# Attention scores from 64 stacked rows per head instead of 128 with zeros, and the mask of the second tile added by VectorE

## What is computed

```
x = x + moe0(pool(x))          # layer 0: masked softmax pooling, 32 experts, 4 a token, and a shared one
y = x @ W[cat] + b[cat]        # layer 1: a matrix per item
q, k, v = split(layernorm(y) @ Wqkv);  q, k = rope(q), rope(k)          # 16 heads of 16
p = softmax(where(k_pos <= q_pos, q @ k.T / 4, -1e9))                   # 256 x 256 per head
y = y + (p @ v) @ Wproj
x = x + y + moe1(layernorm(y)) # 8 experts, 2 a token
```

## Time and profile before

| | us |
|---|---|
| median of 3 runs | 1647.37 (1645.69 to 1647.99) |
| the profiled execution, its own time | 1637.57 |
| its span in the profile | 1635.7 |

### The profile page before, as it was taken

How to read it: one execution, slowest core, us unless ns; L and a number is a source line. 1 busy time by engine, 2 the same in 40 slices (tenths; PEclk the granted TensorE clock), 3 DMA queues, 4 the chain that set the end, 5 groups by cost and what they waited for, 6 DMA issues and landing times.

```text
span 1635.7 us, 27557 instructions
## 1 busy us (share of the span) xinstructions
PE 1437.9 (88%) x9777; PEld 1248.5 (76%) x9777; DVE 1033.1 (63%) x2453; ACT 912.9 (56%) x2160; POOL 717.7 (44%) x712
## 2 busy tenths in 40 slices
PE   7988699999999997589869898889865999999996
PEld 5767599999999986466747666667654999999996
DVE  2998367766776757466756776768554555655552
ACT  5876255555555532267756676758744545554552
POOL 0787443344334114433453545644334444544443
PEclk9998799999999998799988998989876999999998
DMA  5410356555655531676575675676533223433312
GB/s 179 136 56 31 84 164 182 154 163 174 180 155 163 147 112 43 111 125 123 115 131 110 112 136 101 114 126 110 94 129 100 73 55 90 97 90 88 52 22 26
DMA packets 139448, 182.00 MB, mean 111 GB/s; under 512 B 22485, under 2 KB 107296, under 8 KB 139312
## 3 DMA queue, kind: packets, MB, share of 16 engines
q1 hardware_dynamic: 110512, 127.23, 31.3%
q0 software_dynamic: 28160, 51.96, 16.0%
q10 hardware_dynamic: 640, 1.05, 0.4%
HBM read 107.28 MB, written 42.08 MB: 91 GB/s over the span
## 4 chain that ended last, share of the span: by engine, by line
PE 67%; DVE 13%; issue 7%; another core or an unknown queue 7%; ACT 3%; POOL 2%; DMA 1%; SPq 1%; ACTq 0%; DVEq 0%; POOLq 0%
PE banks L942 41%; PE banks L1473 4%; PE banks L1430 4%; PE banks L451 3%; PE banks L1526 2%; PE banks L1004 2%; DVE hidden L977 2%; PE banks L1486 2%; PE banks L1447 1%; DVE lo_w L911 1%; DVE rm L1727 1%; DVE X L1695 1%; PE banks L1540 1%; DVE smax L1685 1%
## 5 line engine op out<-in xcount | busy, mean ns | idle before, releaser
L942 PE MATMUL banks<-hi_x,hi_w 128*128 128x320 f32 (+1 forms) x832 | 293.6, 353 | 35.0 <-DVE hidden L977 24.8
L942 PE MATMUL banks<-lo_x,hi_w 128*128 128x320 f32 (+1 forms) x832 | 288.5, 347 | 0.0
L942 PE MATMUL banks<-hi_x,lo_w 128*128 128x320 f32 (+1 forms) x832 | 288.2, 346 | 0.0
L942 PE MATMUL banks<-hi_w,hi_h 128*128 128x256 f32 x896 | 261.4, 292 | 5.9 <-issue 3.5
L884 POOL DMA_INDIRECT xe<-pooled,idx x160 | 155.5, 972 | 228.3 <-PE banks L1004 183.3
L942 PE MATMUL banks<-lo_w,hi_h 128*128 128x256 f32 x896 | 254.1, 284 | 0.0
L942 PE MATMUL banks<-hi_w,lo_h 128*128 128x256 f32 x896 | 254.0, 284 | 0.0
L942 PEld LDWEIGHTS banks<-hi_x,hi_w 128*128 128x128 f32 x832 | 160.2, 192 | 57.8 <-DVE hidden L977 29.7
L1878 POOL DMA_INDIRECT out<-X,tab x64 | 106.7, 1667 | 200.5 <-DVE X L1978 185.9
L1579 ACT ACTIVATE PN<-banks,smax 128x256 f32<-128x256 f32 (+1 forms) x512 | 180.2, 442 | 14.8 <-DVE smax L1685 13.8
L942 PEld LDWEIGHTS banks<-hi_w,hi_h 128*128 128x128 f32 x896 | 171.9, 192 | 7.6 <-issue 5.1
(11 more groups left out here) (186 smaller groups left out, 3101.0 us busy)
## 6 DMA issues: line engine op xcount, KB each, us to landing
w<-in_L_ffn_w SPq DMA_DIRECT2D x96, 256.0 KB, 5.6
done<-res SPq DMA_DIRECT2D x32, 640.0 KB
QS<-parts_qk SPq DMA_DIRECT2D x128, 128.0 KB
BIG<-in_L_ffn_W SPq DMA_DIRECT2D x16, 1024.0 KB
KS<-parts_qk SPq DMA_DIRECT2D x120, 128.0 KB
mask<-in_c_masks SPq DMA_DIRECT2D x16, 257.0 KB, 2.8
pooled<-XF SPq DMA_DIRECT2D x16, 256.0 KB, 3.3
WS<-in_L_cond_W SPq DMA_DIRECT2D x16, 256.0 KB
```

Source lines behind the costliest of these rows:

```text
L942: last = e.matmul(o, a[i], b[j], start=start and k == 0, stop=stop and k == 2, skip_group_check=True)
```

## The change

`KS` loses its second half and its zeros: head s has its 64 rows of `QS` and the same 64 rows of `KS`, and a score matmul works on these 64 rows alone (`half`). The two clearings by GpSimd and their semaphore go; the stacking of k waits in their place for the earlier users of that memory.

The parts are cut anew. Call 0 of a group now issues all scores of the second query tile, four matmuls of 256 columns, for the two heads of a pair alternately in the lower and upper rows, into banks 0 and 1; bank s holds the heads of half s. It has no mask matmul. Calls 1 and 2 each make half s of part 2: a mask matmul of 256 columns and two score matmuls of 128 columns. The head order of the values step follows.

For banks 0 and 1 VectorE adds a mask tile (`masks`, zeros for the first 128 keys and the triangle for the others), writes the negated sum to `PN` and takes its minimum, in one operation for each head. ScalarE's exponentials for these parts read and write `PN`, with scale -1. Call 0 waits for VectorE's four operations on the group before, not for ScalarE. In `PE_ROUND` three steps change places. The eight table entries of a routing group are issued four in each of two items.

```diff
     def stack(e, b, x):
-        if b < 2 and x == 1:
-            e.wait_ge(s_blocks, b + 1)
+        if b == 0 and x == 1:
+            e.wait_ge(s_xe_turned, 3 * E0)
+            for q in range(2):
+                e.wait_ge(s_res_out[q], 16 * (E0 // 2))
+        if b == 1:
             e.wait_ge(s_x_lo, x_count(NPT - 1, 1))
...
-                dst = KS[b % 2][rows_, s, :, :] if x else QS[b % 2][rows_, :, :]
+                dst = (KS if x else QS)[b % 2][rows_, :, :]
     def pe_scores(e, G, part):
-        if G >= 1:
-            e.wait_ge(s_pn, exp_count(G - 1, part))
-        if part < 2:
-            pair = 2 * g + part
-            e.matmul(PS[:, part, :]...[:, :, 1, :], ident_b[:, :], wide(causal[:, :], 1, [P, HQ, P]), start=True, ...)
-            last = e.matmul(PS[:, part, :], QS[b % 2][:, pair, P:T], KS[b % 2][:, :, pair, :], ...)
+        half = lambda t, s: t[b % 2][s * P // HQ:(s + 1) * P // HQ]
+        if part == 0:
+            if G >= 1:
+                e.wait_ge(s_smax, 5 * (G - 1) + 4)
+            for x in range(2):
+                for s in range(HQ):
+                    last = e.matmul(PS[:, s, x * T:(x + 1) * T], half(QS, s)[:, 2 * g + x, P:T], half(KS, s)[:, 2 * g + x, :], ...)
+                    if x == 1:
+                        last.then_inc(s_s[s], 1)
         else:
-            e.matmul(PS[:, 2, :]..., ident_b[:, :], wide(causal[:, :], 1, [P, HG, P]), start=True, ...)
+            s = part - 1
+            if s == 1:
+                e.wait_ge(s_s[2], 2 * G + 1)
+            elif G >= 1:
+                e.wait_ge(s_pn, exp_count(G - 1, 2))
+            e.matmul(PS[:, 2, s * T:(s + 1) * T]..., ident_b[:, :], wide(causal[:, :], 1, [P, 2, P]), start=True, ...)
             for x in range(2):
-                last = e.matmul(PS[:, 2, x * T:(x + 1) * T], QS[b % 2][:, pair, 0:P], KS[b % 2][:, :, pair, 0:P], ...)
+                last = e.matmul(PS[:, 2, (2 * s + x) * P:(2 * s + x + 1) * P], half(QS, s)[:, 2 * g + x, 0:P],
+                                half(KS, s)[:, 2 * g + x, 0:P], ...)
     act_attn, step exp
+                    if part < 2:
+                        e.wait_ge(s_smax, 5 * G + col + x + 1)
+                        e.activation(s, s, ACT.Exp, bias=smax[:, slot, col + x:col + x + 1], scale=-1.0).then_inc(s_pn, 1)
     dve_attn, step row_max
-                    e.wait_ge(s_pn, 8 * (G - NPN + 1))
+                    e.wait_ge(s_pt_ps, 3 * (G - NPN + 1))
+                if part < 2:
+                    for x in range(2):
+                        cols, col = slice(x * T, (x + 1) * T), 2 * part + x
+                        e.tensor_tensor_reduce(PN[:, slot, part, cols], PS[:, part, cols], masks[:, :], -1.0, 3.0e38,
+                                               ALU.add, ALU.min, smax[:, slot, col:col + 1]).then_inc(s_smax, 1)
     PE_ROUND: the order of the steps that move, before and after
-        ("scores", -1, 3, 0), ("turn_p", -1, 2, 2), ("scores", -1, 3, 1), ("values", -1, 1), ("norm_turn", 1),
-        ("turn_p", -1, 2, 0), ("turn_p", -1, 2, 1), ("gate_turn", -2),
+        ("scores", -1, 3, 0), ("turn_p", -1, 2, 2), ("values", -1, 1), ("norm_turn", 1),
+        ("turn_p", -1, 2, 0), ("turn_p", -1, 2, 1), ("scores", -1, 3, 1), ("gate_turn", -2),
-        ("scores", 0, 2, 1), ("matrix", 2),
+        ("matrix", 2), ("scores", 0, 2, 1),
     POOL_FIRST
-        (0, "blocks", 0), ... (0, "blocks", 1)
     pool_attn, step entry
-                for i in range(2 * d[0], 2 * d[0] + 2):     # two scatters a step, in the item where a group ends
+                g, i = entry_at(b, d[0])                    # one scatter a step, in that item and in the next
```

More of the change, by code:

```diff
@@ L126, in _build @@
     QS1 = sb("QS1", [P, NPAIR, T], F32R, place)
-    KS1 = sb("KS1", [P, HQ, NPAIR, T], F32R, place)
+    KS1 = sb("KS1", [P, NPAIR, T], F32R, place)
     place.close()
@@ L1223, in _build @@
     POOL_LAST = (
-        ("base", 14), ("entry", 14, 0), ("entry", 14, 1), ("entry", 14, 2), ("entry", 14, 3), ("norm", 15, 1),
-        ("base", 15), ("entry", 15, 0), ("entry", 15, 1), ("entry", 16, 0), ("entry", 16, 1))
+        *(("entry", 13, i) for i in range(TB * K1)), ("base", 14), *(("entry", 14, i) for i in range(R * K1)), ("norm", 15, 1), ("base", 15),
+        *(("entry", 15, i) for i in range(TB * K1)), *(("entry", 16, i) for i in range(TB * K1)))
     SP_LAST = (
@@ L1279, in group_ended, with entry_at @@
         return group_begun(b - 1) if b > 0 else None
+    def entry_at(b, i):
+        if group_ended(b) is not None:
+            return group_ended(b), i
+        return (group_ended(b - 1), TB * K1 + i) if group_ended(b - 1) is not None else None
     LBANK = 6
@@ L1326, in sp_attn @@
         wait_routed(e)
-        for dst, src in ((causal_f[:, :], io["c_causal"]),
+        for dst, src in ((masks[:, :], io["c_causal"]),
                          (wqkv[:, :, :], io["L1_ffn_WqkvT"].rearrange("(c p) f -> p c f", p=P)),
@@ L1390, in pool_attn @@
         for step, b, d in rounds(POOL_FIRST, POOL_ROUND, POOL_LAST):
[L1391 to L1395, removed]
+            if step == "got":
                 t, k = d
@@ L1413, in pool_attn @@
                                 ALU.add).then_inc(s_base, 1)
-            elif step == "entry" and group_ended(b) is not None:
-                g = group_ended(b)
-                t0 = r1.tiles(g)[0]
+            elif step == "entry" and entry_at(b, d[0]):
+                g, i = entry_at(b, d[0])
+                tt, k = r1.tiles(g)[0] + i // K1, i % K1
                 if d[0] == 0:
@@ L1440, in pe_scores @@
                 e.wait_ge(s_stack[x], N_STACK * (b + 1))
-        if G >= 1:
-            e.wait_ge(s_pn, exp_count(G - 1, part))
-        if part < 2:
-            pair = 2 * g + part
[L1445 to L1448, removed]
-        else:
-            e.matmul(PS[:, 2, :].rearrange("p (h k) -> p h k", h=HG), ident_b[:, :], wide(causal[:, :], 1, [P, HG, P]),
-                     start=True, stop=False, skip_group_check=True)
+        half = lambda t, s: t[b % 2][s * P // HQ:(s + 1) * P // HQ]
[4 more added lines that the diff above has]
+                for s in range(HQ):
+                    last = e.matmul(PS[:, s, x * T:(x + 1) * T], half(QS, s)[:, 2 * g + x, P:T], half(KS, s)[:, 2 * g + x, :],
+                                    start=True, stop=True, skip_group_check=True)
+                    if x == 1:
+                        last.then_inc(s_s[s], 1)
+        else:
+            s = part - 1
[3 more added lines that the diff above has]
+                e.wait_ge(s_pn, exp_count(G - 1, 2))
+            e.matmul(PS[:, 2, s * T:(s + 1) * T].rearrange("p (h k) -> p h k", h=2), ident_b[:, :],
+                     wide(causal[:, :], 1, [P, 2, P]), start=True, stop=False, skip_group_check=True)
             for x in range(2):
[L1453 to L1456, removed]
+                last = e.matmul(PS[:, 2, (2 * s + x) * P:(2 * s + x + 1) * P], half(QS, s)[:, 2 * g + x, 0:P],
+                                half(KS, s)[:, 2 * g + x, 0:P], start=False, stop=True, skip_group_check=True)
+            last.then_inc(s_s[2], 1)
     def pe_turn_p(e, G, part):
```

69 lines of the change are left out of this document (32 added, 37 removed).

## The result

The changed kernel took 1695.8 us (median of 4, 1692.5 to 1700.1) beside 1646.5 us for the kernel before in the same session: ratio 1.0305, 95% interval 1.0274 to 1.0336. It is slower by 49 us, twice the 24.5 us of the forecast and inside its range; the rival "all calls are paid" had 1689.

What follows compares the result with a forecast made beforehand. TensorE was taken to bound about half of each attention item. Paid work of 1.35 us plus VectorE's 0.18 made 1.53 us an item, 24.5 us over 16; added to 1647.37 that gave 1672 us, 8-in-10 range 1640 to 1703.

Steps and rivals of the forecast that it cites:

- all calls are paid: Rival: no score call's added TensorE work hides in idle time; 41 us slower, 1689 us; chance 0.10.
- New work on TensorE: Score calls in attention: a group costs 1.735 us against 1.13, so +0.60 us a group.
- A way in and out: TensorE going to 64-row matmuls and back at each score call: 0.325 us lost, ends 0.30 and 0.35.
- Pairs run at once: Call 0: matmuls on upper and lower rows overlap, streaming 0.22 us instead of 0.43.
- the rival without pairs: Rival: call 0's matmuls run one after the other, 0.43 us; +7 us, 1679 us; chance 0.14.
- the 0.27 of a recorded length: Alternative drain price for each of 24 added shape changes on TensorE: 0.27 us, 6.5 us an item.
- Which of it is paid: TensorE's added work: 1.35 us an item paid, 1.05 hidden in VectorE's stretch and the standstill.
- the granted clock: TensorE's clock in attention: a mean of 0.92 was read in the first window; no term priced a change.
- the whole forecast of 1.53: Added time an item in attention: 1.35 us of TensorE plus 0.18 of VectorE, 24.5 us over 16 items.
- VectorE and ScalarE: Attention row maxima and exponentials: VectorE's combined operations add 0.18 us an item on the chain, ScalarE nothing.
- The moved steps save none: TensorE's new round: 32 shape changes an item against 8, and moving steps avoids none of the added ones.
- GpSimd and the transfers: Removed key-tile clearings and moved table entries: worth nothing; without cover 7 us and some 5 us.

Runs made afterwards that it cites:

- the two balances: Profiles of the changed kernel against the kernel before, compared over fifteen items in two sessions: 1695.8 beside 1646.5 us, and 1697.8 beside 1649.3 us.
- the pair without a lower clock: Two variants of the changed kernel: every score matmul on 128 rows, 1508.6 us, and 64-row matmuls with TensorE's round from the kernel before, 1578.1 us.
- the extra one: The changed kernel with a small full-array matmul of 32 columns between the two pairs of call 0: 1559.4 us, ratio 1.0377 to the kernel before.
- all rows: The changed kernel with every score matmul on 128 rows, two heads' scores added up: 1509.2 us, ratio 1.0046 to the kernel before; run again, 1508.6 us, 1.0027.
- third batch: A later session of follow-up kernels, in which the kernel before took 1503.4 us.
- the second pair: The changed kernel and the kernel before, both unchanged, profiled again in a later session: 1697.8 beside 1649.3 us, ratio 1.0291.
- the kernel with this part alone: The kernel before with only VectorE adding the mask of parts 0 and 1, TensorE's two masks gone: 1500.5 us, ratio 0.9981; again 1501.4 us, 0.9981.
- the first pair: The changed kernel and the kernel before, profiled in the original session: 1695.8 beside 1646.5 us, ratio 1.0305.
- the old order: The changed kernel with TensorE's round of the kernel before: 1578.1 us, ratio 1.0503 to the kernel before.

## Why the prediction was right in its sign, and half in its size

- **New work on TensorE: right.** +0.60 us a group was forecast; the two balances give 34.5 and 35.5 us over sixty groups and the pair without a lower clock 35.8, 0.6 each. A way in and out was priced at 0.325 (0.30 to 0.35); the extra one measured 0.29.
- **Pairs run at once: right.** Call 0 takes 0.43 us to the next start for four matmuls on halves, and 0.56 on 128 rows (*all rows* of the third batch, below). One after the other they were to stream for 0.43 alone, with the way on top. So the rival without pairs is out.

```profile
1008.50 0.72 PE L1444 MATMUL banks<-KS,QS 128*128 128x256 f32 x4
1009.06 0.60 PE L1477 MATMUL banks<-ident,PN 128*128 128x128 f32 x4
```

- **Where the loss sits.** The low calls cost some 33 us and call 0 some 6. By TensorE's line (typical values of the stage), four transposes, call 0 and four transposes take 0.53 + 0.43 + 0.49 = 1.45 us with the halves and 0.36 + 0.56 + 0.44 = 1.36 with 128 rows: the pairs pay for most of their own way. Calls 1 and 2 take 0.57 from the mask on where they take 0.29 with 128 rows: they pay the same way for two matmuls of 128 columns in which nothing runs at once. The Trainium skill, TensorEngine Tiling (Array Packing), Key Properties, says that a change of the tiling mode drains TensorE; the rows agree that each change costs, at 0.29 / 2 = 0.15 us, and not the 0.27 of a recorded length by which 6.5 us an item were worked out.
- **Which of it is paid: the step that went wrong.** The forecast let the work of group 0 and of half of group 1, 1.05 us an item, disappear in VectorE's stretch and in the standstill. The two pairs of profiles show TensorE's idle time down by 0.44 and 0.87 us an item, so 0.2 to 0.6 more was paid. The wait for VectorE of 24.0 us fell to 4.5, and the waits at the outputs step went from 34 to 46 us. In the second pair, read over the same fifteen items, the first fell from 10.5 to 3.0 and the others from 48 to 44, so how the idle time divides among the waits differs from profile to profile. What both pairs show is that work put beside a standstill did not shorten the idle time by the same amount. Why is not shown.
- **A term that was missing: the granted clock.** It was read (0.92 and 0.80 in the earlier trace rows) and then held constant. It fell from 0.91 to 0.88 and from 0.92 to 0.89, which is some 1.5 and 1.4 us an item of slower work (estimates), about as large as the whole forecast of 1.53. The balance is 2.3 + 1.5 - 0.4 = 3.3 us in the first pair and 2.4 + 1.4 - 0.9 = 2.9 in the second. The split between work and clock rests on taking half of the busy time at the lower level for slowness; the 2.4 us of the pair without a lower clock bears it out. This is the larger of the two errors. That the total came out inside the range, near the rival with all calls paid, is luck: that rival reached 1689 with no clock in it.
- **VectorE and ScalarE: right that they cost nearly nothing.** 0.18 us an item was forecast on the path; the kernel with this part alone is not slower than before, in the batches without standstills. VectorE has 7 us more in fifteen items, where some 12 over the whole were forecast.
- **The order: half seen.** "The moved steps save none" of the changes is true (31 changes with the old order, 32 with the new), but the wait that they avoid, 1.9 us an item, was not looked for. The prediction listed what frees banks 0 and 1 and said nothing of call 1, which had come to wait for the bank of the third part.
- **GpSimd and the transfers.** Their parts were not run by themselves; the kernels with all rows bound them, together with the split of the third part into two calls, at 4 to 7 us.

What stays open: why the idle time gives up so little, why the stretches at the lower level are longer in the changed kernel, and why the standstills are absent where before takes 1503 us.

## What to carry to other kernels

Count the changes between tile shapes in the order of TensorE, not only the columns that a smaller shape saves: at 0.29 us in and out a 64-row step must save more than that, and the two matmuls of 128 columns here could not. When TensorE's work is added beside a pause, price the clock too, since most pauses here were followed by microseconds at half speed, and let idle time absorb no more than the traces show it to have given. When a call is given another bank, look at every place of the order for who frees that bank.

## What the runs showed of the hardware

One more change between 64-row and 128-row matmuls and back costs 0.29 us, even around one record of 32 columns. In one item, after a standstill of 3.4 us, TensorE worked for 5.5 us without a gap at the lower level before the full one came back. And the same kernel, before, ran in 1503 us in two batches and in 1649 us in another. The profiles of its nearest relatives show most of the difference in TensorE's idle time and clock in the attention stage, and some 50 us ahead of it: the first item's XR starts at 682 to 692 us where before takes 1503 us, and at 731 to 741 us where it takes 1647 to 1649. The cost of this change was 36 to 44 us (estimated) where before takes 1503 us, and 48.5 us where it takes 1649.
